# Where the next batch's x is split, and how the projections are cut into pieces, in a fused attention and feed-forward kernel

## What is computed

```python
q = (x @ Wq).reshape(B, T, 16, 32); k = ...; v = ...
scores = jnp.einsum('bthd,bshd->bhts', q, k) * tril
attn = softmax(scores / T ** 0.5)
out = jnp.einsum('bhts,bshd->bthd', attn, v).reshape(B, T, 512)
x = _layernorm(x + out @ Wo)
```

## Time and profile before

| | |
|---|---|
| median of 3 runs | 1098.29 us (1097.52 to 1098.69) |
| the profiled execution | 1098.31 us, its span 1096.6 us |
| busy in the span | PE 1038.9, DVE 738.8, ACT 485.6, POOL 293.6 us |
| attention | to about 415 us |
| batch 0, 1, 2, 3 | unit 0 begins at 35.5, 133.2, 232.8, 331.8 us |

### The profile page before, as it was taken

One profiled execution on the slowest core, in us unless ns is written; L12 is line 12 of the kernel. 1 busy time (PEld: TensorE's weight loads), 2 busy tenths in 40 slices (PEclk: granted clock), 3 DMA queues, 4 the chain that ended last, 5 costly groups with the idle time before them and its releaser, 6 DMA issues.

```text
span 1096.6 us, 18098 instructions
## 1 busy us (share of the span) xinstructions
PE 1038.9 (95%) x6022; PEld 838.8 (76%) x6023; DVE 738.8 (67%) x1768; ACT 485.6 (44%) x904; POOL 293.6 (27%) x496
## 2 busy tenths in 40 slices
PE   7889998999999885999999999999999999999995
PEld 6667776777777664888888888888888888888884
DVE  6898699778868886556757546545665535654766
ACT  5788488658857883223324222131222122222125
POOL 2186347445733741222220006000000000000224
PEclk9999999999999998999999999999999999999998
DMA  8887267727743832224541004210020001100112
GB/s 261 235 197 205 75 202 208 186 93 179 202 108 118 216 129 77 70 85 155 182 161 60 1 1 40 38 39 1 1 77 24 15 0 38 38 1 1 39 39 77
DMA packets 55217, 106.19 MB, mean 97 GB/s; under 512 B 6240, under 2 KB 8288, under 8 KB 55136
## 3 DMA queue, kind: packets, MB, share of 16 engines
q1 hardware_dynamic: 50256, 90.99, 30.3%
q0 software_dynamic: 4880, 14.18, 3.5%
HBM read 72.11 MB, written 30.94 MB: 94 GB/s over the span
## 4 chain that ended last, share of the span: by engine, by line
PE 60%; DMA 0%; DVE 0%; issue 0%; ACT 0%; POOLq 0%; POOL 0%; ACTq 0%; DVEq 0%
PE f_bank L42 57%; PE f_bank L1655 1%; PE f_bank L1663 1%; PE f_bank L1725 1%; PE f_bank L1679 0%; DMA rows<-sorted_dram 0%; POOLq L1429 0%; POOL out L1601 0%; ACT rows_kept L1086 0%; ACTq L1429 0%; DVE ln_stats L1058 0%; DVE gt_lo L1922 0%; DVE rows_kept L2051 0%; ACT gt_hi L1806 0%; DVE ln_mv L1060 0%
## 5 line engine op out<-in xcount | busy, mean ns | idle before, releaser
L1828 ACT ACTIVATE fsg<-f_bank 128x512 f32<-128x512 f32 x64 | 38.2, 597 | 299.6 <-PE f_bank L42 299.4
L1978 DVE TENSOR_TENSOR h<-f_bank,fsg 128x512 f32<-128x512 f32 x64 | 44.2, 691 | 182.4 <-PE f_bank L42 182.3
L699 ACT ACTIVATE probs<-bank,nmax 128x384 f32<-128x384 f32 (+3 forms) x256 | 131.5, 548 | 21.8 <-DVE nmax L876 19.8
L860 DVE CUSTOM_DVE_ANT_0 bank<-bank,mask 128x384 f32<-128x384 f32 (+3 forms) x256 | 123.1, 503 | 14.0 <-PE bank L495 13.1
L506 PE MATMUL bank<-ident,probs 128*128 128x128 f32 x640 | 108.7, 284 | 24.2 <-DVE pt_lo L885 11.1
L1091 POOL TENSOR_SCALAR ln_var<-ln_mv 128x1 f32<-128x1 f32 x39 | 8.9, 229 | 442.6 <-DVE ln_mv L1060 441.3
L885 DVE TENSOR_TENSOR pt_lo<-bank,pt_hi 128x512 f16<-128x512 f32 (+1 forms) x192 | 114.9, 599 | 16.7 <-ACT pt_hi L709 16.4
L709 ACT ACTIVATE pt_hi<-bank 128x512 f16<-128x512 f32 (+1 forms) x192 | 104.8, 546 | 23.8 <-PE bank L506 23.3
L42 PE MATMUL bank<-x_hi,w_qk 128*128 128x512 f32 x256 | 101.0, 412 | 6.5 <-DVE x_lo L890 6.1
L42 PE MATMUL f_bank<-wd_hi,hs_hi 128*128 128x512 f32 x256 | 99.9, 390 | 0.8 <-issue 0.8
L42 PE MATMUL f_bank<-wd_hi,hs_lo 128*128 128x512 f32 x256 | 99.8, 390 | 0.0
(11 more groups left out here) (262 smaller groups left out, 2464.8 us busy)
## 6 DMA issues: line engine op xcount, KB each, us to landing
big_lo<-q_hi_dram SPq DMA_DIRECT2D x32, 256.0 KB, 4.2
big_lo<-q_lo_dram SPq DMA_DIRECT2D x32, 256.0 KB, 4.8
big_lo<-k_hi_dram SPq DMA_DIRECT2D x32, 256.0 KB, 3.9
big_lo<-k_lo_dram SPq DMA_DIRECT2D x32, 256.0 KB, 5.3
rows<-sorted_dram SPq DMA_DIRECT2D x19, 256.0 KB, 2.7
q_hi_dram<-q_hi SPq DMA_DIRECT2D x16, 256.0 KB, 3.0
q_lo_dram<-q_lo SPq DMA_DIRECT2D x16, 256.0 KB, 3.4
k_hi_dram<-k_hi SPq DMA_DIRECT2D x16, 256.0 KB, 3.7
```

Of the source, the lines that this page charges most:

```text
L699: ins = act.activation(probs[u % RP][:, at:at + cols(r)], S[u % SR][:, at:at + cols(r)], ACT.Exp, bias=nmax[:, r, c:c + 1])
L860: dve.tensor_tensor_reduce(out=S[u % SR][:, at:at + cols(r)], in0=S[u % SR][:, at:at + cols(r)], in1=mask[:, T - cols(r):T], scale=1.0, sc ...
L1828: act.activation(fsg[v % 2][:, :], GB[v % 2][:, :], ACT.Silu).then_inc(s_sg, 1)
L1978: dve.tensor_tensor(h[r % 2][:, j, :], UB[v % 2][:, :], fsg[v % 2][:, :], ALU.mult).then_inc(s_h, 1)
```

## The change

The pieces of the projections get two tables, one for batches 0 to 2 and one for the last batch. In batches 0 to 2 groups 8 to 11 begin earlier and the last three go in six pieces of two matmuls. In the last batch groups 4 to 7 go in five pieces of three or two. The four splits of the next batch's x move to units 18 to 21, and each waits, instead of for the whole of group 7, for the values that TensorE makes behind the piece of group 7 that reads the same block. GpSimd's remainders of x move one head forward, the first store of padding moves from head 5 to head 8, the routing steps leave out units 18 to 26, and two of the turns of the last batch move.

```diff
-        even, brief, wide = (3, 3, 3, 3), (4, 4, 4), (3, 2, 2, 2, 3)
-        groups = {4: (2, even, 6), 5: (7, brief, 10), 6: (11, even, 15), 7: (16, even, 21),
-                  8: (27, even, 31), 9: (32, even, 36), 10: (37, wide, 42), 11: (43, even, 48)}
-        pieces = {}
-        for g, (first, sizes, _) in groups.items():
-            for i, n in enumerate(sizes):
-                pieces[first + i] = (g, sum(sizes[:i]), sum(sizes[:i]) + n)
-        split_at = {at: g for g, (_, _, at) in groups.items()}
-
-        x_split_at = {22: 0, 24: 1, 25: 2, 27: 3}
+        even, brief, wide, long = (3, 3, 3, 3), (4, 4, 4), (3, 2, 2, 2, 3), (2,) * 6
+        XT_FROM = 16
+        groups = {4: (2, even, 6), 5: (7, brief, 10), 6: (11, even, 15), 7: (XT_FROM, even, 20),
+                  8: (22, even, 26), 9: (27, long, 33), 10: (34, long, 40), 11: (41, long, 48)}
+        last_groups = {4: (2, wide, 7), 5: (8, wide, 13), 6: (14, wide, 19), 7: (20, wide, 25)}
+
+        def piece_table(table):
+
+            return {first + i: (g, sum(sizes[:i]), sum(sizes[:i]) + n)
+                    for g, (first, sizes, _) in table.items() for i, n in enumerate(sizes)}
+
+        def split_table(table):
+            return {at: g for g, (_, _, at) in table.items()}
+
+        pieces = [piece_table(last_groups), piece_table(groups)]
+        split_at = [split_table(last_groups), split_table(groups)]
+
+
+        x_split_at = {XT_FROM + 2 + k: k for k in range(KT)}
...
-        SPLIT_FROM, SPLIT_TO = 21, 30
+        SPLIT_FROM, SPLIT_TO = 18, 27
...
-        turn_at = {25: 0, 33: 1, 46: 2}
+        turn_at = {27: 0, 34: 1, 46: 2}
...
-        x_lo_in_front = {6: (0,), 7: (1, 2)}
-        x_lo_behind = {7: (3,)}
-        pads_at = (5, 9, 10)
-        x_lo_met = (24, 27, 30)
+        x_lo_in_front = {5: (0,), 6: (1, 2), 7: (3,)}
+        pads_at = (8, 9, 10)
+        x_lo_met = (24, 27)
...
-                        for k in x_lo_behind.get(c, ()) if more else ():
-                            x_lo(b + 1, k)
...
-                    if u in pieces and (more or pieces[u][0] < 2 * NM):
-                        project(b, *pieces[u])
+                    if u in pieces[more]:
+                        project(b, *pieces[more][u])
...
-                    if u in split_at and (more or split_at[u] < 2 * NM):
-                        split_proj(b, split_at[u])
+                    if u in split_at[more]:
+                        split_proj(b, split_at[more][u])
                     if more and u in x_split_at:
-                        if x_split_at[u] == 0:
-
-                            act.wait_ge(s_pj, (b + 1) * 2 * NM)
+
+                        act.wait_ge(s_pv, b * UPB + XT_FROM + x_split_at[u] + AHEAD_V + 1)
                         x_split(b + 1, x_split_at[u])
```

## The result

| | before | changed |
|---|---|---|
| median, us | 1098.39 (1097.52 to 1098.72, 8 runs) | 1101.89 (1100.66 to 1104.32, 8 runs) |
| ratio, 95% interval | | 1.003 (1.0022 to 1.0039) |
| the profiled execution, span, clock | 1098.31, 1096.6, 0.992 | 1100.99, 1099.3, 0.991 |

A forecast was written before the change was run, and what follows sets the result against it. The late stage holds the chain; attention before it moves it, paced at units 20 to 26 by ScalarE's in-order queue. Batches 0 to 2 +1.14, x_lo +1.6, batch 1 -0.58, last batch +0.4: 1100.9 us, range 1096.3 to 1103.2.

The forecast's parts named there:

- Two splits ahead of the copy in unit 20: Batches 0 to 2: group 7's and an x split delay the copy; T(27), start of unit 27's transposes, moves +1.65 us.
- Splits at 18 and 19 for nothing: Batches 0 to 2: splits of x beside three-matmul units cost nothing; 0.52 us each without that cover.
- x_lo late in batch 0, +1.6: Batch 0: TensorE waits for GpSimd's x_lo cuts, 0.5 in unit 23, 1.1 in unit 25; +1.6 us, bounds 0 and 3.
- T(27) to T(47) of 28.88: Batches 0 to 2: groups 9 to 11 in two-matmul pieces take 28.88 us against 30.38, -1.50.
- +0.23 behind T(47): Batches 0 to 2: values of unit 46 wait longer for pt_lo: +0.23 us, bounds 0 and 0.47.
- -0.58 in batch 1: Batch 1, unit 32: a routing step no longer stands behind a split: -0.58 us, bounds -0.6 and 0.
- Last batch +0.4: Last batch: T(2) to T(25) +0.1, k stack late for the scores issued in unit 33 +0.3; +0.4 us.
- The sum: Whole kernel: 1.14 + 1.6 - 0.58 + 0.4 = +2.6 us on 1098.31, giving 1100.9 us; chance 0.42.
- GpSimd in time: Rival: no x_lo wait in batch 0, and the last stack in time; 1.9 falls away, 1099.0 us; chance 0.27.
- Spreading in full: Rival: all batches, two-matmul units at TensorE's own pace, no DVE waits behind splits; 9.4 us less, 1091.5; chance 0.13.
- Last stack late: Rival: last batch, the k stack for unit 33 costs +2.2 us instead of 0.3; 1102.8 us; chance 0.11.
- Port held: Rival: four other two-element nmax a batch meet a cut, 0.24 us more each; +2.9, 1103.8 us; chance 0.07.

The follow-up runs named there:

- last experiment: Changed kernel with the nmax of unit 33 issued element by element in batches 0 to 2: 1100.74 us, ratio 1.0018.
- last but one experiment: On the kernel with Wo's cuts later and groups' splits at u mod 3 = 0: last x split at 24, not 23, group 8 five pieces; 1093.27 us.
- the splits moved: Changed kernel with the last two splits of x at units 22 and 23 instead of 20 and 21: 1100.11 us, ratio 1.0008.
- both edits: Changed kernel with splits of x at 18, 19, 22 and 23 and GpSimd's cuts of Wo behind heads 9 to 12: 1096.85 us, ratio 0.9982.

## Why the prediction was right, step by step

- **Two splits ahead of the copy in unit 20, T(20) to T(27) from 10.22 to 11.87**: right, 11.89 in batches 1 and 2. Unit 20 took 0.85 more (0.84 forecast), unit 26 1.80 (1.79). The cause is shown by taking one split out (-0.51 in unit 20), by taking the other out (1.50 with a split of x alone) and by the copy's change of place (+0.16, not less).
- **Splits at 18 and 19 for nothing**: right. T(0) to T(20) stayed within 0.01 in batches 0 to 2.
- **x_lo late in batch 0, +1.6**: right, in the units named, 0.48 and 1.22 over batch 2's lengths (0.5 and 1.1 forecast). It goes when the cuts of Wo stand later, so the queue is the cause. The last cut's old start, 79.19, stands in the earlier trace rows and not in the earlier trace rows, as the prediction has it.
- **T(27) to T(47) of 28.88**: the lengths of the two-matmul units held (4.38 for 4.37), but the sum was 0.37 too long: batch 2 took 28.51. Most of it is unit 35, 1.28 and not 1.47 (its copy starts 0.01 before T(35) instead of 0.2 behind it, so the exponentials are ready sooner), and units 39 to 41, 4.52 against 4.63.
- **+0.23 behind T(47)**: 0.23 to 0.25 in the three batches.
- **-0.58 in batch 1**: T(27) to T(47) fell by 2.24 there and by 1.87 in batch 2, so -0.37. The stretch still takes 0.21 more than in batch 2: two of batch 1's routing steps now meet GpSimd's scaling and last 0.83 and 0.45 us. The bound (-0.6 to 0) holds it.
- **Last batch +0.4**: +0.16. T(2) to T(25) took 34.98 (35.19 before; 35.3 forecast), units 25 to 32 11.30 (11.3 forecast), and the scores issued in unit 33 were 0.15 late at most. Here the sum had a hole: its own 11.3 is 0.52 more than the 10.78 that these units took before (371.44 to 382.22 in the earlier trace rows), and no term stands for it. From T(33) to T(47) 0.15 was gained. So -0.21, +0.52 and -0.15 make the +0.16, and the forecast's +0.1 and +0.3 name neither part. The forecast of the stack had a write-to-read gap of 3.0 or more; here it was 2.06, but one pair of reads took 2.35 to issue. SyncE in the last batch:

```profile
375.41 0.34 SPq L406 DMA_DIRECT2D k_lo_dram<-k_lo  x1
377.47 0.79 SPq L415 DMA_DIRECT2D big_lo<-k_hi_dram  x2
378.30 2.35 SPq L415 DMA_DIRECT2D big_lo<-k_lo_dram  x2
```

- **The sum**: +2.6 forecast, +2.55 in the trace's batches and +2.8 to +3.5 in the two medians. That it is so near is luck: errors cancel. Batch 2 came out 0.35 below its forecast, and so did batch 1 by 0.14 and the last by 0.24, while batch 0 came out 0.72 above. There T(27) to T(47) fell by 0.88 only and not by 1.50. Of the 0.92 that it takes more than in batch 2, 0.56 is the nmax held by GpSimd. With that gone (last experiment) units 28 to 31 still take 0.16 more than in batch 2 and units 33 and 34 together 0.23, with DVE doing 98 instructions against 90 in the stretch of the changed kernel. A routing step of 0.79 us, held like the nmax, stands in unit 30; what each step costs was not taken apart.
- **The rivals.** GpSimd in time: no. Spreading in full: three two-matmul units take 4.38, so no; but in the version without the two waits the kernel is 5.4 us faster than before, of which the early splits of x alone gave 1.3. What the pieces and what the other moves give of the rest was not taken apart. Last stack late: by 0.15 us in the profiled execution; by 0.99 in that of another kernel with the same last batch (last section). Port held: the mechanism is there, at another place than named. No two-element nmax met a cut of x_lo or Wo. Seven met sums of heads or scalings of o_raw and lasted 0.28 to 0.96 us, but seven lasted 0.29 to 0.40 in the kernel before too; new is the one of 0.96, 0.8 more than alone and not 0.24, since the price I took from the earlier trace rows was one sample of how much of the other's instruction was left.

## What to carry to other kernels

In a software pipeline where one engine goes in order, look for the instruction that the bottleneck waits for (here the exponentials behind the last head's copy) and keep everything movable out of the queue between its trigger and itself: one of two splits, 0.5 us of ScalarE, cost unit 20 its 0.5 us in each batch, and in units 22 and 24, which have no copy, nothing (last but one experiment). A split that doesn't wait for the same late result as the copy can be over in time and be free there too (1.50 against 1.47). Two delays at one place cover each other, so an edit alone may show nothing there (batch 0: 74.71 us with the splits moved, 74.68 without, 71.82 with both edits). A queue moved forward in steady state has to be read again in the first batch, where one-off work stands in the same queue.

## What the hardware showed that was not expected

- **A short wait, and half the clock behind it.** In the kernel with the cuts of Wo moved, the last stack came late in the profiled execution, the scores of unit 33 waited 0.99 us, and the granted clock went to half, from 2.4 to 1.2 GHz:

```profile
385.68 0.76 PE L501 MATMUL bank<-big_lo 128*128 128x384 f32 x2 [0.99 <-issue]
```

```profile
384.06:386.83 2.77, 1.78 (x15) 1.48 (x15) 0.85 (x5) 1.60 (x3) 0.14 (x1) 0.70 0.99 299
386.83:389.35 2.52, 2.52 (x16) 2.21 (x14) 2.11 (x9) 1.09 (x2) 0.09 (x1) 0.50 1.04 398
389.35:390.98 1.63, 1.43 (x13) 1.14 (x12) 1.31 (x4) 1.39 (x4) 0.92 (x3) 0.50 1.05 397
```

Units 33 and 34 took 2.77 and 2.52 us, where the changed kernel took 1.16 and 1.61 at full clock; the whole batch 72.06 instead of 68.94. Ahead of it TensorE had been busy 8.10 of 11.30 us in the changed kernel's row. In two traces the fall came right behind such a wait, and once, in batch 0 of the kernel with the cuts of Wo moved (above), behind two units without a projection. The same two units stand in the other traces of batch 0 with no fall behind them. That the wait is the cause was not isolated.
- **GpSimd's instruction holds a two-element one of DVE to its end**: 0.96 us for an instruction of 0.16, and 73 of 73 such meetings in fourteen traces. One-element forms pass, and beside GpSimd's `rinv` nothing was held.
- **The start moves.** T(0) of batch 0 lay between 35.1 and 37.5 us in the fourteen traces, which is as much as the effect under study; hence the comparisons by lengths between the transposes.
